# Differential attention with a routed expert layer: score tiles of two heads' 64 query rows, nine kinds of chunk instead of five

## What is computed

```python
s1 = jnp.einsum('bhqd,bhkd->bhqk', q, k1) * SCALE     # and s2 with k2; both causal
attn = softmax(s1) - lam * softmax(s2)                # lam = sigmoid(lambda_logit), by head
attn = attn / jnp.maximum(jnp.sum(jnp.abs(attn), axis=-1, keepdims=True), 1e-06)
x = layernorm(x + (attn @ v) @ Wo.T)
```

## Time and profile before

| | |
|---|---|
| time, median of 3 runs | 1171.25 us (1169.71 to 1172.33) |
| the profiled execution's own time | 1169.67 us |
| its span, first to last instruction | 1167.9 us |
| mean granted TensorE clock | 0.866 of 2.4 GHz |
| first score matmul, last score matmul | 43.2 us, 1018 us |
| DMA, mean over the span | 119 GB/s |

### The profile page before, as it was taken

How to read it: one execution, slowest core, us unless ns; L and a number is a source line. 1 busy time by engine, 2 the same in 40 slices (tenths; PEclk the granted TensorE clock), 3 DMA queues, 4 the chain that set the end, 5 groups by cost and what they waited for, 6 DMA issues and landing times. The chain is left out here.

```text
span 1167.9 us, 27864 instructions
## 1 busy us (share of the span) xinstructions
PE 923.4 (79%) x8522; PEld 734.2 (63%) x8522; DVE 951.3 (81%) x2449; ACT 843.1 (72%) x2706; POOL 839.1 (72%) x1120
## 2 busy tenths in 40 slices
PE   2478778878898789988897988977898888868581
PEld 1255555657677677757676766756676767757571
DVE  1499998879998899889998999889988999825132
ACT  1499988678888788787878878887878878723130
POOL 3388977797768987688768977798769976851503
PEclk9587887669999898888999899989988889968786
DMA  3703500533246524662347414652347322236562
GB/s 101 176 2 92 109 1 15 137 97 116 80 142 158 170 72 127 170 193 69 103 125 181 154 54 155 159 178 91 111 121 187 113 91 83 79 127 190 175 209 60
DMA packets 117045, 139.38 MB, mean 119 GB/s; under 512 B 11042, under 2 KB 99490, under 8 KB 116898
## 3 DMA queue, kind: packets, MB, share of 16 engines
q1 hardware_dynamic: 112802, 129.21, 38.3%
q0 software_dynamic: 4096, 8.40, 2.4%
HBM read 107.81 MB, written 29.75 MB: 118 GB/s over the span
## 5 line engine op out<-in xcount | busy, mean ns | idle before, releaser
L697 ACT ACTIVATE exps<-scores,neg_max 128x512 f32<-128x512 f32 (+3 forms) x1024 | 541.8, 547 | 118.3 <-DVE neg_max L988 113.7
L988 DVE TENSOR_REDUCE neg_max<-scores 128x1 f32<-128x512 f32 (+3 forms) x896 | 424.1, 525 | 56.4 <-PE scores L1118 50.4
L623 POOL TENSOR_SCALAR exps<-exps,inv_l,lam_l 128x384 f32<-128x384 f32 (+3 forms) x448 | 278.6, 628 | 94.9 <-DVE inv_l L963 82.7
L627 POOL TENSOR_TENSOR exps<-exps 128x512 f32<-128x512 f32 x256 | 325.8, 1273 | 21.4
L1150 PE MATMUL trans<-ident,exps 128*128 128x128 f32 x1280 | 238.5, 316 | 116.9 <-ACT diffT L704 65.5
L1116 PE MATMUL scores<-stack 72*128 72x512 bf16 (+3 forms) x1024 | 277.2, 339 | 16.1 <-DMA stack<-parts_dram 15.6
L1150 PEld LDWEIGHTS trans<-ident,exps 128*128 128x128 f32 x1280 | 159.9, 159 | 180.0 <-issue 98.9
L697 ACT ACTIVATION_READ_ACCUMULATOR exps<-scores,neg_max 128x1 f32 x1024 | 231.7, 226 | 0.0
L704 ACT ACTIVATE diffT<-trans 128x512 f32<-128x512 f32 x320 | 195.4, 611 | 46.3 <-PE trans L1150 44.6
L998 DVE TENSOR_REDUCE abs_sum<-exps 128x1 f32<-128x512 f32 (+3 forms) x448 | 223.2, 521 | 6.4 <-POOL exps L627 6.4
L1118 PE MATMUL scores<-causal_bf,ident_bf 128*128 128x128 bf16 x1024 | 212.3, 240 | 0.0
(11 more groups left out here) (138 smaller groups left out, 911.7 us busy)
## 6 DMA issues: line engine op xcount, KB each, us to landing
w_sb<-w_dram SPq DMA_DIRECT2D x120, 512.0 KB
stack<-parts_dram SPq DMA_DIRECT2D x288, 96.0 KB
parts_dram<-parts SPq DMA_DIRECT2D x104, 128.0 KB, 2.4
xg<-x_sorted_dram SPq DMA_DIRECT2D x24, 256.0 KB
y_sorted_dram<-y_sorted SPq DMA_DIRECT2D x24, 256.0 KB
x_in<-x_dram SPq DMA_DIRECT2D x8, 256.0 KB, 4.7
x_res<-x_dram SPq DMA_DIRECT2D x8, 256.0 KB, 4.5
o_dram<-y_out SPq DMA_DIRECT2D x8, 256.0 KB, 2.3
```

Of the source, the lines that this page charges most:

```text
L623: nc.gpsimd.tensor_scalar(diff[:, ring, col:col + w], exps[:, ring, 1, col:col + w], inv_l2[:, i:i + 1], lam_l1[:, i:i + 1], ALU.mult, ALU ...
L627: nc.gpsimd.tensor_tensor(diff[:, ring, :], diff[:, ring, :], exps[:, ring, 0, :], ALU.subtract)\
L697: nc.scalar.activation(exps[:, ring, k, col:col + w], scores[:, c % 2, k, col:col + w], ACT.Exp, bias=neg_max[:, c % 2, k, i:i + 1], accum ...
L988: nc.vector.tensor_reduce(neg_max[:, c % 2, k, i:i + many], scores[:, c % 2, k, col:col + many * w].rearrange("p (i w) -> p i w", w=w), AX ...
```

## The change

A unit is now 64 query rows of **two** heads: the rows of one head fill PSUM partitions 0 to 63, those of the other 64 to 127. Tile j of 64 rows (0 to 7) needs (j + 1) x 64 keys. A group of four heads has 16 units, packed in nine chunks of 512 columns: 512; 448 + 64; 384 + 128; 320 + 192; 256 + 256; 512; 448 + 64; 384 + 128; 320 + 192. A batch has 36 chunks and 36 slots. With it:

- PE's scores: for each unit and score two matmuls with 64 columns of the array (for j = 2 four, so that its key blocks lie where PV wants them), then the causal one over all 128 partitions, 64 columns. PV: 64 query columns a matmul, twice as many; key blocks of 128 that may begin in the middle of a tile (`KEY_BLOCKS`), for which a second copy of the values, shifted by 64 tokens, is kept. It is made by two DMAs on SP's queue after ACT's copy of the values, and DVE's spreading of the values reads both. The values of a batch are its last preparation task. The transpose of the denominators is 32 matmuls instead of 4 transposes.
- DVE makes the difference for kinds 0 and 5 (eight chunks a batch, as before), POOL for the other 28, not 32. Reciprocals and lam products come in five sets a group, where two pairs had six.
- Absolute sums lag four slots, not five; diffT's ring is 9 chunks, not 12; PV visits are five a group (`PV_STEPS`), 20 a batch as before. The guard step of the denominators and its reciprocal move down within DVE's slot. All side tables are written anew for 36 slots.
- Before the first batch DVE makes four small copies (lam by pair, the causal triangle for both halves), and POOL one more memset.

The diff, cut to what the steps below speak of:

```diff
-LAG_ABS = 5
+LAG_ABS = 4
-EXP_RING, DIFF_RING = 7, 12
+EXP_RING, DIFF_RING = 7, 9
-DVE_KINDS = (0,)
-PAIR_CHUNKS = (((3, 0, 0),), ((2, 0, 0), (0, 0, 384)), ((1, 0, 0), (1, 1, 256)), ((3, 1, 0),), ((2, 1, 0), (0, 1, 384)))
+DVE_KINDS = (0, 5)
+HALF = P // 2
+KINDS = 9
+ROWS_OF = (((7, 0, 0),), ((6, 0, 0), (0, 0, 448)), ((5, 0, 0), (1, 0, 384)), ((4, 0, 0), (2, 0, 320)),
+           ((3, 0, 0), (3, 1, 256)),
+           ((7, 1, 0),), ((6, 1, 0), (0, 1, 448)), ((5, 1, 0), (1, 1, 384)), ((4, 1, 0), (2, 1, 320)))
+SLOTS = NG * KINDS
-SUM_SETS = {1: (0, 3, 1), 2: (3, 8, 4), 4: (4, 7, 1)}
+SUM_SETS = {1: (0, 3), 3: (3, 7), 4: (7, 9), 6: (9, 12), 8: (12, 16)}
+PV_STEPS = {4: (3,), 5: (7,), 6: (6, 0), 7: (5, 1), 8: (4, 2)}
+KEY_BLOCKS = {7: ((0, 0), (1, 1), (2, 2), (3, 3)), 6: ((0, 0), (1, 1), (2, 2), (3, NT + 2)), 5: ((0, 0), (1, 1), (2, 2)),
+              4: ((0, 0), (1, 1), (2, NT)), 3: ((0, 0), (1, 1)), 2: ((2, NT + 3), (3, 0)), 1: ((3, 0),), 0: ((3, NT + 1),)}
-HIDDEN_SLOTS = (45, 47, 49, 51, 53, 55, 59, 60, 64, 66, 68, 70, 72, 74, 76)
-EXPERT_SLOTS = (48, 50, 52, 54, 56, 58, 62, 63, 67, 69, 71, 73, 75, 76, 78)
+HIDDEN_SLOTS = (42, 42, 45, 48, 50, 51, 54, 55, 59, 60, 62, 64, 66, 68, 69)
+EXPERT_SLOTS = (43, 45, 48, 51, 52, 53, 57, 58, 61, 63, 65, 67, 69, 69, 71)
-SCATTER_SLOTS = (31, 32, 33, 34, 35, 36, 37, 38)
+SCATTER_SLOTS = (29, 30, 30, 31, 32, 32, 32, 34)
-PREP_SLOTS = (15, 18, 23, 24, 25)
+PREP_SLOTS = (14, 16, 20, 21, 22)
...
+                            sp.wait_ge(v_evacuated.sem, v_evacuated.after(n, 1))
+                            sp.dma_start(v_next[0:HALF, NT:2 * NT:2, :], v_next[0:HALF, 2:NT, :]).then_inc(v_shifted.sem, 16)
+                            sp.dma_start(v_next[HALF:P, NT + 1:2 * NT:2, :], v_next[0:HALF, 0:2, :]).then_inc(v_shifted.sem, 16)
...
-                            for t, pair, second, col, _ in units_of(c):
-                                w = (t + 1) * P
-                                h = QUAD * g + 2 * (pair % 2) + second
-                                nc.tensor.matmul(scores[:, c % 2, k, col:col + w], stack[:, 0, h, t * P:(t + 1) * P],
-                                                 stack[:, 1 + k, h, 0:w], start=True, stop=False)
-                                last = nc.tensor.matmul(scores[:, c % 2, k, col + w - P:col + w], ident_bf[:, :],
-                                                        causal_bf[:, :], start=False, stop=True)
+                            for j, pair, col, _ in units_of(c):
+                                w = (j + 1) * HALF
+                                for s in range(2):
+                                    rows, h = slice(s * HALF, (s + 1) * HALF), QUAD * g + 2 * (pair % 2) + s
+                                    queries = stack[:, 0, h, j * HALF:(j + 1) * HALF]
+                                    if j == 2:
...
+                                    else:
+                                        nc.tensor.matmul(scores[rows, c % 2, k, col:col + w], queries,
+                                                         stack[:, 1 + k, h, 0:w], start=True, stop=False, skip_group_check=True)
+                                own = col if j == 2 else col + w - HALF
+                                last = nc.tensor.matmul(scores[:, c % 2, k, own:own + HALF], ident_bf[:, :],
+                                                        causal_half[:, :], start=False, stop=True, skip_group_check=True)
                             last.then_inc(score_done.sem, 1)
...
+                        for j in PV_STEPS[c % GROUP]:
+                            for at, (block, i) in enumerate(KEY_BLOCKS[j]):
                                 for k in range(QUAD):
...
+                                    col = (block + 2 * (j == 3 and k >= 2)) * P + k % 2 * HALF
                                     last = nc.tensor.matmul(
-                                        heads[k * STRIP:(k + 1) * STRIP, t * P:(t + 1) * P], v_sb[:, i, NG * k + g, :],
-                                        diffT[:, ring_d(n, source), col:col + P],
+                                        heads[k * STRIP:(k + 1) * STRIP, j * HALF:(j + 1) * HALF], v_sb[:, i, NG * k + g, :],
+                                        diffT[:, ring_d(n, source), col:col + HALF],
```

More of the change, by code:

```diff
@@ L100, in units_of @@
+PREP_SLOTS = (14, 16, 20, 21, 22)
 def units_of(c):
[L102 to L110, removed]
+    g, kind = divmod(c, KINDS)
+    for j, par, col in ROWS_OF[kind]:
+        yield j, 2 * g + par, col, 2 * NT * 2 * g + QUAD_UNITS.index((j, par))
 def reductions(c):
-    kind = c % KINDS
@@ new lines, in body @@
+                    for n, c in chunks(b, stages, slot, LAG_EXP):
+                        ring = ring_e(n, c)
+                        m, used = earlier(n, c, EXP_RING)
+                        act.wait_ge(*diff_ready(m, used))
+                        act.wait_ge(max_done.sem, max_done.after(n, maxima_done(c, 0)))
+                        for i, (j, _, col, place) in enumerate(units_of(c)):
+                            w = (j + 1) * HALF
+                            nc.scalar.activation(exps[:, ring, 0, col:col + w], scores[:, c % 2, 0, col:col + w],
+                                                 ACT.Exp, bias=neg_max[:, c % 2, 0, i:i + 1],
+                                                 accum_out=sums[:, 0, place:place + 1]).then_inc(exp_done.sem, 1)
@@ new lines, in body @@
+                    for n, c in chunks(b, stages, slot, LAG_COPY):
+                        m, used = earlier(n, c, DIFF_RING)
+                        act.wait_ge(trans_done.sem, trans_done.after(n, c + 1))
+                        act.wait_ge(pv_done.sem, pv_done.after(m, pv_done_for(used)))
+                        nc.scalar.activation(diffT[:, ring_d(n, c), :], trans[:, :], ACT.Copy)\
+                            .then_inc(diffT_copied.sem, 1)
+                    for n, c in chunks(b, stages, slot, LAG_EXP):
+                        ring = ring_e(n, c)
+                        m, used = earlier(n, c, EXP_RING)
+                        act.wait_ge(trans_done.sem, trans_done.after(m, used + 1))
+                        act.wait_ge(abs_done.sem, abs_done.after(m, REDUCTIONS[used + 1]))
+                        act.wait_ge(max_done.sem, max_done.after(n, maxima_done(c, 1)))
+                        for i, (j, _, col, place) in enumerate(units_of(c)):
+                            w = (j + 1) * HALF
+                            nc.scalar.activation(exps[:, ring, 1, col:col + w], scores[:, c % 2, 1, col:col + w],
+                                                 ACT.Exp, bias=neg_max[:, c % 2, 1, i:i + 1],
+                                                 accum_out=sums[:, 1, place:place + 1]).then_inc(exp_done.sem, 1)
@@ L979, in body @@
                                                            op0=ALU.mult, op1=ALU.subtract).then_inc(diff_dve_done.sem, 1)
+                    for n, c in chunks(b, stages, slot, LAG_DEN):
+                        if (c + 1) % (SLOTS // 2) == 0:
+                            i = (c + 1) // (SLOTS // 2)
+                            half = slice((i - 1) * UNITS // 2, i * UNITS // 2)
+                            dve.wait_ge(abs_done.sem, abs_done.after(n, REDUCTIONS[c + 1]))
+                            nc.vector.scalar_tensor_tensor(out=guard[:, half], in0=sums[:, 0, half], scalar=DENOM_MIN,
+                                                           in1=abs_sum[:, half], op0=ALU.mult, op1=ALU.max)\
+                                .then_inc(den_done.sem, 1)
                     route(b, stages, slot, 1)
```

246 lines of the change are left out of this document (120 added, 126 removed).

## The result

The changed kernel takes 1323.14 us (median of 4 runs, 1309.07 to 1329.48) where the kernel before takes 1170.48. The ratio of comparable runs is 1.1225 (95% interval 1.1178 to 1.1272): 12% slower. The direction was forecast, the size was not: 1216 was predicted, and 1262 was the end of the range. A repeat of four runs has a median of 1326.32 us and a recorded ratio of 1.1362 (1.1287 to 1.1437). In both series two of the four executions (1329 to 1335 us, mean granted clock 0.792 to 0.798) are disturbed ones beside the other two (1309 to 1319 us, 0.808 to 0.816), and the repeat's 1.1362 is more than its undisturbed two alone give: 1314.5 us in the mean over 1168.89 before, 1.125.

A forecast was written before the change was run, and what follows sets the result against it. DVE was taken to bound the kernel before, PE the changed one: six batches at +5.3 us and +14 for the first make +46, so 1169.7 becomes 1216 us. The range was 1124 to 1262 us, the forecast's own case 1180 to 1262.

The forecast's parts named there:

- What bounds before, and PE's need: Kernel before: DVE sets the slot, busy 92% of a 129.7 us batch; PE needs 94 us at full clock.
- 25.5 more PE: PE per batch: scores +26.4 us, transposes -1.8, PV +0.1, denominator transposes +0.8, raising need from 94 to 119.5.
- The halves run together; alternating forms drains the array at 64 columns too: PE scores: concurrent halves, 15.4 us of columns, plus 0.28 us for each of 128 unit-scores; 51.2 us, +26.4 a batch.
- Rival (a): PE scores: alternating array forms is free, DVE stays the bound at 124.4 us a batch; 1127 us, chance 0.21.
- rival (c): PE scores: the halves run in turn, 15.4 us more a batch, 155 us a batch; over 1300 us, chance 0.03.
- PV and transposes: PE per batch: sixteen transposes fewer, -1.8 us; PV 160 groups at 0.055 us, +0.1, with 20 visits as before.
- DVE: DVE work per batch: fewer columns in maxima and absolute sums, fewer reciprocals, wider V copy; -4.8 us, 119.2 to 114.4.
- Order and queues: Slots, lags and DMA queues: moved absolute sums, smaller ring, V shift and tail cost 0; setup copies under 1 us.
- The sum: Whole run: PE bounds at 130 us, 135 with stalls; six batches +5.3 us, first +14, second none; +46, 1216 us.
- The allowance for stalls: PE in later batches: 96% busy because of waits for POOL and ACT, making a batch 135 us, +5.3.
- rival (b): PE clock: drains are paid, but a fuller PE gets clock 1.00 and fits under DVE; 1150 us, chance 0.16.
- The chances: Whole run: slower 0.56, same 0.07, faster 0.37; the forecast's own case, 1180 to 1262 us, 0.53.

The follow-up runs named there:

- e1: The changed kernel with each causal matmul split into two 64-column halves, so all scores of a chunk keep one array form; 1177.27 us, ratio 1.0149 to the kernel before.
- e2: The kernel before with only each causal matmul split into two 64-column halves, so the array changes form around it; 1289.95 us, ratio 1.1107.
- e3: The changed kernel with causal matmuls last in two-unit chunks, 72 form changes a batch for 128, output wrong, timing only; 1236.02 us, ratio 1.0661.
- e4: The changed kernel plus two useless 256-column matmuls ahead of each slot's transposes; 1283.65 us, ratio 1.1079 to the kernel before.
- e10: The changed kernel plus four useless 256-column matmuls ahead of each slot's transposes; 1322.17 us, ratio 1.1329 to the kernel before.

## Why the prediction was right in sign and wrong in size

*What bounds before, and PE's need.* Right. The 94 us of need counted by starts carried the whole argument: with 25.5 more PE took over, as the chain, the busy shares and DVE's waits show. One reading is off without weight: the third and the eighth batch before take 122.5 and 125.6 us, outside the 127.4 to 131.1 that the prediction gives from the third on.

*The halves run together; alternating forms drains the array at 64 columns too.* Right, by the pitches: 0.255 us for a unit-score, where 0.28 was taken, 48 us of scores a batch where 51.2 stood. Rival (a), free alternation at 1127, and rival (c), halves in turn at 1300 and more, are both refuted by the same rows, although (c)'s time lies near the measured one. A time alone would have confirmed the wrong story. The Trainium skill (TensorEngine Tiling (Array Packing), Tiling Modes) states the drain; the trace agrees, and e1, e2 and e3 give its price. The twofold speed of 64-wide tiles, which the prediction places under Performance Considerations, is stated on that page under Theoretical Speedup; the trace agrees (0.34 us for two halves of 0.213 and a change of form). The 24 us that the prediction gives for scores without the drains should by its own terms be 51.2 - 128 x 0.24 = 20.5; nothing hangs on it.

*PV and transposes.* Right: PV's 40 narrow matmuls from 906.88 to the transposes at 907.57 are 0.69 us, ten groups at 0.055 and the way out of the form.

*DVE.* 116.6 to 117.6 us in the four batches from 454.6 us, 116.9 in the mean, forecast 114.4: of the 4.8 us that DVE was to save, 2.3 came. Some of its instructions take longer though their shape did not change: the two of the norms, `xh` and `x_twice`, 534 and 432 ns in the mean where they took 348 and 340, and those of `hit` from `probs` and `rank`, 1056 and 656 ns where they took 128 and 464. These four groups alone are 2.4 us a batch. Why they lengthen is not shown. PE bounds here, so it is off the path; in e1 it is not.

*Order and queues.* The four-slot lag of the absolute sums brings 3.7 us of waits in the whole run (6.4 before), and no wait for the V shift or the smaller ring appears. Taken at 0, right. The fill is 2.6 us longer (forecast under 1) and the tail 6.5 shorter (forecast 0); no run follows these up.

*The sum: here it failed.* The step is "119.5 us at full clock, 130 at the present 0.92", and for the first two batches the division by 0.81 and 0.75. Both take the granted clock of the kernel before for that of the changed one. The measured clock is 0.56 in the first two batches and 0.87 to 0.90 in the five after them. The allowance for stalls, 96% busy, failed beside it: in those five PE is recorded busy 94%, idle 9.2 us of a batch of 144.9 on average (311.5 to 1035.9 us). The batches came to +144 us, not +46. Of the 98 us between, the first two make 41 (55 us more than before, where 14 was forecast) and the other six 57.

For the first two the clock is the cause, by an estimate from the rows. The division by the clock has a fault of its own there: only columns stretch with it, while a change there and back goes from 0.23 to 0.25 us. The need of these batches is 83.8 us at full clock (the forecast's 86.8 less the 3 by which the drains were overpriced). Divided whole by 0.56 that would be 150 us, more than either took (121.2 and 143.7). Of it 34 us are drains (128 x 0.23 and 20 x 0.24) and 50 are columns: 50 / 0.56 + 37 = 126 us for each in the mean, and PE is recorded busy 127 on average. At the forecast's 0.81 and 0.75 the same sum gives 97 and 102. e2 has the same fall of clock and the same 55 us from the alternation alone.

For the other six the split stays an estimate. The same sum with 116.5 us of need (82.5 of columns, 34 of drains) gives 129 us at 0.88, and 134 with the 96%; at 0.92 it gives 124 and 129 to 130. So the lower clock is worth 4 to 5 us of a middle batch that took 145. Some 11 us remain for waits and for what the count leaves out: PE is recorded busy 136 us there, 7 more than the sum gives. How they divide is open.

The thought that would have caught the clock stood in rival (b), "a drain is no work, so the columns per slot hardly rise", and was used only against a higher clock. It spoke as well for a lower one: in the batches with the least work for PE, where the clock was 0.81 and 0.75, PE was about to get some 40% more time (25.5 us on 61) with no more columns.

*The chances.* 0.56 for slower was right and too low for what the rows of the drains showed; the range ended at a clock of 0.88 everywhere and left out the first two batches' fall.

## What to carry to other kernels

Before putting small tiles into a stream of full-array matmuls, count the changes of form: here each way there and back costs 0.2 to 0.3 us, for 32-wide and 64-wide tiles alike, and 128 of them in a batch cost PE some 27 us (128 x 0.21) where the new chunks saved DVE 2.3. If tiles are used, everything between two drains should take the same form, also the matmul that does not need it (e1). And when PE becomes the bound, the columns in its need must be divided by the clock that it will then be granted, which fell here when the added time was drains (0.81 to 0.56 and 0.61 in the first batch of the changed kernel and of e2). The drains themselves are not to be divided.

## What was not expected of the hardware

The granted clock can stay low while PE is recorded busy without a gap. Two stretches of the changed kernel:
```profile
131.40:233.80 102.40, 102.30 (x985) 59.69 (x984) 72.98 (x197) 67.06 (x228) 58.93 (x84) 0.50 0.23 50
892.60:957.50 64.90, 59.45 (x806) 42.13 (x804) 61.07 (x165) 50.14 (x169) 49.55 (x68) 1.00 0.37 112
```
102 us at 1.2 GHz with PE busy 102.30 us, and 65 us at 2.4 GHz with PE busy 92% of the time. The record of busy time hides a difference: in the first PE alternates without a single expert matmul between, in the second it streams 104 of them as well. The fillers, which add columns, lift the clock from 0.811 to 0.88 and 0.90 in the mean (e4, e10), and e10's 15.4 us a batch of them on the bounding engine (about 120 us in all) lengthen the run by 10 us. At half clock a change of form there and back costs 0.25 us instead of 0.23, while the columns take twice as long.
